# Two draining slots of a software pipeline written out by hand, with a new order on four engines

## Reference, cut to what matters

```python
h = _layernorm(x) * (1 + ca) + sa
# eight times, with weights of the layer:
q, k, v = h @ Wq + bq, h @ Wk + bk, h @ Wv + bv
Q, K = elu(q) + 1, elu(k) + 1
KV, Ksum = (K * v).sum(rows), K.sum(rows)
V = Q * KV / (Q * Ksum + EPS_Z)
h = _layernorm(gelu(V @ Wo + bo) + h, ln1)
h = _layernorm(gelu(gelu(h @ Wf1 + bf1) @ Wf2 + bf2) + h, ln2)
# behind the layers:
x = x + ga * h
h = _layernorm(x) * (1 + cb) + sb
x = x + gb * (shared(h) + sum over the 2 best of 8 experts)
```

## Time and profile before

| | |
|---|---|
| median of 3 runs (lowest, highest) | 519.76 us (519.69, 519.83) |
| profiled execution, its own time | 519.92 us |
| its span, first to last instruction | 518.1 us |
| busy PE / DVE / ACT / POOL | 97% / 82% / 74% / 48% |
| granted TensorE clock, mean | 1.000 |

### The profile page before, as it was taken

The page is one execution under the profiler, slowest core; times in us unless marked ns, Lnnn a source line. Parts: engine busy times, 40 slices in busy tenths (PEclk is TensorE's granted clock), DMA queues, the critical chain, the costliest instruction groups (busy, mean ns, idle before and its releaser), DMA issues.

```text
span 518.1 us, 7999 instructions
## 1 busy us (share of the span) xinstructions
PE 502.8 (97%) x1933; PEld 299.1 (58%) x1933; DVE 423.4 (82%) x1624; ACT 384.7 (74%) x570; POOL 247.1 (48%) x291
## 2 busy tenths in 40 slices
PE   8789999999999999999999999999989999999997
PEld 6345555555555556555555555555555566666664
DVE  5888888988898888888888888898887656876754
ACT  4768888888888888888888888888887753545332
POOL 3445555566556566655556655566655530201000
PEclk9999999999999999999999999999999999999999
DMA  8200010001000000100010001000000000707070
GB/s 246 95 16 1 7 41 15 0 5 41 15 5 20 20 15 5 40 16 0 5 41 15 5 0 41 15 5 20 20 1 1 2 0 13 171 0 184 1 184 20
DMA packets 19527, 17.51 MB, mean 34 GB/s; under 512 B 8605, under 2 KB 14237, under 8 KB 19509
## 3 DMA queue, kind: packets, MB, share of 16 engines
q1 hardware_dynamic: 18644, 16.58, 12.4%
q10 hardware_dynamic: 864, 0.73, 0.4%
HBM read 9.96 MB, written 1.05 MB: 21 GB/s over the span
## 4 chain that ended last, share of the span: by engine, by line
PE 87%; DVE 5%; POOL 3%; issue 2%; ACT 2%; DMA 1%; DVEq 0%; POOLq 0%
PE bank L442 19%; PE bank L433 15%; PE bank L308 12%; PE bank L598 7%; PE bank L455 6%; PE bank L430 5%; PE bank L350 4%; PE bank L355 4%; PE bank L351 4%; PE bank L558 3%; PE bank L557 3%; PE bank L556 3%; DVE hf L1042 1%; PE bank L554 1%; DVE stI L1006 1%
## 5 line engine op out<-in xcount | busy, mean ns | idle before, releaser
L442 PE MATMUL bank<-hid,wf 128*128 128x512 f32 x256 | 120.2, 592 | 0.0
L915 POOL TENSOR_TENSOR rsD<-veD,c_half 128x4 f32<-128x4 f32 x32 | 37.8, 1180 | 118.0 <-DVE veD L1023 118.0
L433 PE MATMUL bank<-x,wf 128*128 128x512 f32 x192 | 93.0, 593 | 0.0
L758 ACT ACTIVATE hid<-bank,vbf 128x512 f32<-128x512 f32 x128 | 77.6, 693 | 1.9 <-PE bank L433 1.9
L442 PEld LDWEIGHTS bank<-hid,wf 128*128 128x128 f32 x256 | 46.1, 190 | 46.6 <-issue 31.3
L433 PEld LDWEIGHTS bank<-x,wf 128*128 128x128 f32 x192 | 35.0, 189 | 33.3 <-issue 16.3
L1113 DVE TENSOR_SCALAR x<-bank,vln 128x256 f32<-128x256 f32 x64 | 31.9, 540 | 23.8 <-PE bank L308 23.8
L1042 DVE TENSOR_SCALAR xhB<-bank,meanB,rsB 128x128 f32<-128x128 f32 x128 | 43.7, 404 | 9.2 <-POOL rsB L915 9.2
L1042 DVE TENSOR_SCALAR xhD<-bank,meanD,rsD 128x128 f32<-128x128 f32 x128 | 43.7, 404 | 7.2 <-POOL rsD L915 2.9
L728 ACT ACTIVATE g<-bank,vbf 128x512 f32<-128x512 f32 x31 | 21.4, 690 | 35.8 <-PE bank L442 35.8
L308 PEld LDWEIGHTS bank<-ident,y 128*128 128x128 f32 x256 | 29.5, 140 | 26.3 <-POOL y L935 12.9
(11 more groups left out here) (175 smaller groups left out, 1087.9 us busy)
## 6 DMA issues: line engine op xcount, KB each, us to landing
wf<-in_w_f SPq DMA_DIRECT2D x16, 256.0 KB, 2.6
hid<-kv_full SPq DMA_DIRECT2D x12, 256.0 KB, 4.2
x<-kv_full SPq DMA_DIRECT2D x9, 256.0 KB, 5.0
wu<-in_w_unit SPq DMA_DIRECT2D x10, 192.0 KB
wqkv<-in_w_qkv SPq DMA_DIRECT2D x7, 192.0 KB, 2.3
x<-in_x SPq DMA_DIRECT2D x4, 256.0 KB, 5.5
qk<-kv_full SPq DMA_DIRECT2D x3, 256.0 KB, 4.9
out<-ot SPq DMA_DIRECT2D x3, 256.0 KB, 2.2
```

Source lines behind the costliest of these rows:

```text
L433: mm = nc.tensor.matmul(ps_ff[j][:], wf1[:, j * P:(j + 1) * P], x2[(c - 2) % CH][:], start=True, stop=True)
L442: mm = nc.tensor.matmul(ps_f0[:], wf2[:, j, :], hid[:, j, :], start=(j == 0), stop=(j == FJ - 1))
L758: nc.scalar.activation(hid[:, j, :], ps_ff[j][:], ACT.Gelu_apprx_tanh, bias=vbf1[:, j:j + 1]).then_inc(h_ready, 1)
L915: nc.gpsimd.tensor_tensor(rs[buf(k, n)][:], ve[buf(k, n)][:], c_half[:], ALU.pow).then_inc(rstd_ready[k], 1)
```

## The change

The last slot of the loop and the two draining slots are no longer written by `slot`:

- ScalarE: the table of Ln, Ln and dd of item 31 come directly behind the gelus of slot 31, with the last norm of item 28 between them (it was at the end of slot 31), then zf; the gelu g2 of item 29, which stood ahead of them, comes behind. The weight splits and the second norm stand at other places of the stream.
- DVE: the end of slot 31 (normalize of B for item 30, and rk) is written behind rk and nck; x2 comes behind vt; y1 of item 31 is added on DVE instead of POOL; the statistics of F come ahead of those of B, those of D for item 29 behind them.
- TensorE: Wo of item 31 goes into ps_v instead of ps_b and stands ahead of ff1 of item 30; y1's transposes go into ps_v, the hidden norm of chunk 0 into ps_b (`fm_bank`); the transposes of y2 (item 29) come behind ff1(0), those of its normalized rows in the next slot, behind the scores; the scores stand within ff1 of item 31; the transposes of y2 of item 30 come behind ff2(1) of item 31, and those of its normalized rows behind ff2(3). All `keep_awake` calls here are gone.
- POOL: three of the roots, the sums, h_lo and the low parts in a new order, without y1.

The diff, without its blank lines:

```diff
@@ -115,6 +115,10 @@
         first_bank = [ps_f0, ps_f1, ps_f0, ps_d]
         gate_bank, up_bank = [ps_k, ps_f1], [ps_b, ps_f0]
+        def fm_bank(c):
+            return ps_v if c else ps_b
         def gates(i):
@@ -504,12 +508,12 @@
             def norm_to_fm(c):
                 pe.wait_ge(normed["F"], c + 1)
                 if c == 0:
-                    pe.wait_ge(kv_ready, NI)
+                    pe.wait_ge(x2_ready, HB * last)
                 if c:
                     pe.wait_ge(cst_ready, c)
                 if c == 2:
                     pe.wait_ge(x_ready, NI + CH)
-                transposes(ps_v, xh["F"], to_fm["F"])
+                transposes(fm_bank(c), xh["F"], to_fm["F"])
             def scores(c):
                 pe.wait_ge(hf_ready, c + 1)
@@ -561,6 +565,7 @@
                 c, u = divmod(i, U)
                 if i == 0:
                     pe.wait_ge(hf_ready, 1)
+                    pe.wait_ge(x2_ready, HB * NI)
                 if c == 0 and i >= FIRST:
                     pe.wait_ge(wu_hi_ready, i - FIRST + 1)
                     pe.wait_ge(wu_lo_ready, i - FIRST + 1)
@@ -578,8 +583,6 @@
             def up(i):
                 c, u = divmod(i, U)
-                if i == 0:
-                    pe.wait_ge(x2_ready, HB * NI)
                 if i == 1:
                     pe.wait_ge(g2_ready, NI)
                 if i >= 2 and i - 2 < U:
@@ -625,15 +628,68 @@
                 gate(0)
                 up(0)
-            slot(NI, 0, LAYERS, {"start": lambda: zf_to_tm(0)})
+            def sum_to_tm(d):
+                pe.wait_ge(y2_ready, d + 1)
+                pe.wait_ge(x_ready, d + CH)
+                transposes(ps_d, y2, to_tm["D"])
+            def rows_to_fm(d):
+                pe.wait_ge(normed["D"], d + 1)
+                transposes(ps_d, xh["D"], to_fm["D"])
+            def inner(f, j):
+                if j == 0:
+                    pe.wait_ge(g2_ready, f)
+                if j == 3:
+                    pe.wait_ge(k_ready, NI)
+                    pe.wait_ge(h_ready, FJ * f)
+                if j == 2:
+                    for h in range(HB):
+                        pe.wait_ge(x2_ready, HB * f + h + 1)
+                        mm = nc.tensor.matmul(half(ps_ff[2], h), wf1[:, 2 * P:3 * P], half(x2[f % CH], h),
+                                              start=True, stop=True)
+                else:
+                    mm = nc.tensor.matmul(ps_ff[j][:], wf1[:, j * P:(j + 1) * P], x2[f % CH][:],
+                                          start=True, stop=True)
+                mm.then_inc(ff1_mm, 1)
+            def outer(f, js):
+                for j in js:
+                    pe.wait_ge(h_ready, FJ * f + j + 1)
+                    mm = nc.tensor.matmul(ps_f0[:], wf2[:, j, :], hid[:, j, :], start=(j == 0), stop=(j == FJ - 1))
+                if j == FJ - 1:
+                    mm.then_inc(ff2_mm, 1)
+            pe.wait_ge(normed["B"], last)
+            transposes(ps_b, xh["B"], to_fm["B"])
+            zf_to_tm(0)
+            pe.wait_ge(v_ready, NI)
             pe.wait_ge(kv_ready, NI)
-            keep_awake(12, ps_v)
-            def awake_0():
-                keep_awake(4, ps_v)
-            slot(NI + 1, 1, LAYERS, {"start": awake_0, "within ff1": lambda: norm_to_fm(0),
-                                     "behind ff2": scores_0, "behind the last norm": unit_0})
+            nc.tensor.matmul(ps_v[:], wo[:], vt[CH - 1][:], start=True, stop=True).then_inc(wo_mm, 1)
+            inner(last - 1, 2)
+            inner(last - 1, 0)
+            pe.wait_ge(y1_ready, NI)
+            transposes(ps_v, y1, to_tm["B"])
+            sum_to_tm(last - 2)
+            inner(last - 1, 1)
+            inner(last - 1, 3)
+            outer(last - 1, (0, 1, 2, 3))
+            pe.wait_ge(normed["B"], NI)
+            transposes(ps_v, xh["B"], to_fm["B"])
+            norm_to_fm(0)
+            inner(last, 2)
+            inner(last, 0)
+            scores_0()
+            rows_to_fm(last - 2)
+            inner(last, 1)
+            inner(last, 3)
+            outer(last, (0, 1))
+            sum_to_tm(last - 1)
+            outer(last, (2, 3))
+            rows_to_fm(last - 1)
+            unit_0()
             for i in range(CH * U):
@@ -765,7 +821,7 @@
                         run(extra, "before the last norm")
                     if j == 3 and has(a) and splits_next(s, c):
                         split_qkv_hi(l + 1)
-                    if j == 3 and has(d) and has(b):
+                    if j == 3 and has(d) and has(b) and has(s + 1):
                         last_norm(c, d)
                         if has(s + 1):
                             act.wait_ge(v_mm, d + 1)
@@ -788,7 +844,7 @@
                 act.wait_ge(to_fm["F"], c + 1)
                 for h in range(HB):
                     b = c * HB + h
-                    ev = nc.scalar.activation(half(hf[c], h), half(ps_v, h), ACT.Identity,
+                    ev = nc.scalar.activation(half(hf[c], h), half(fm_bank(c), h), ACT.Identity,
                                               bias=mod[:, 3, b:b + 1], scale=m1[:, 1, b:b + 1])
                 ev.then_inc(hf_ready, 1)
@@ -846,22 +902,42 @@
                 for u in us:
                     nc.scalar.activation(wu_hi[:, u, 0:2, :], wu[:, u, 0:2, :], ACT.Copy).then_inc(wu_hi_ready, 1)
-            def first_rows():
-                second_norm(0)
-                split_h_hi(0)
-            def last_splits():
-                split_weights_hi(ORDER[7:])
-                scaled(1)
+            def outer_gelu(f):
+                act.wait_ge(ff2_mm, f + 1)
+                nc.scalar.activation(g2[:], ps_f0[:], ACT.Gelu_apprx_tanh, bias=vbf2[:, 0:1]).then_inc(g2_ready, 1)
+            def inner_gelu(f, j):
+                act.wait_ge(ff1_mm, FJ * f + (2, 3, 1, 4)[j])
+                nc.scalar.activation(hid[:, j, :], ps_ff[j][:], ACT.Gelu_apprx_tanh,
+                                     bias=vbf1[:, j:j + 1]).then_inc(h_ready, 1)
+            nc.scalar.preload_act_table_set(LN_SET)
+            act.wait_ge(q_ready, NI)
+            nc.scalar.activation(lden[:], qk[:], ACT.Ln, bias=c_eps[:, 0:1]).then_inc(lden_ready, 1)
+            last_norm(CH - 1, NI - CH)
+            act.wait_ge(lden_ready, NI)
+            nc.scalar.activation(dd[:], lden[:], ACT.Exp, bias=c_lneps[:, 0:1], scale=-1.0).then_inc(dd_ready, 1)
             scaled(0)
-            slot(NI, 0, LAYERS, {"after the first gelu": lambda: split_weights_hi(ORDER[:3]),
-                                "before the last norm": lambda: split_weights_hi(ORDER[3:5]),
-                                "end": lambda: split_weights_hi(ORDER[5:7])})
-            slot(NI + 1, 1, LAYERS, {"start": lambda: norm_rows(0), "after the first gelu": first_rows,
-                                     "before the last norm": last_splits})
-            act.wait_ge(ff2_mm, NI)
-            nc.scalar.activation(g2[:], ps_f0[:], ACT.Gelu_apprx_tanh, bias=vbf2[:, 0:1]).then_inc(g2_ready, 1)
+            outer_gelu(NI - 3)
+            act.wait_ge(wo_mm, NI)
+            nc.scalar.activation(g1[:], ps_v[:], ACT.Gelu_apprx_tanh, bias=vbo[:, 0:1]).then_inc(g1_ready, 1)
+            for j in range(FJ):
+                inner_gelu(NI - 2, j)
+            norm_rows(0)
+            outer_gelu(NI - 2)
+            second_norm(0)
+            split_h_hi(0)
+            split_weights_hi(ORDER[:2])
+            inner_gelu(NI - 1, 0)
+            last_norm(0, NI - 3)
+            for j in range(1, FJ):
+                inner_gelu(NI - 1, j)
+            split_weights_hi(ORDER[2:5])
+            scaled(1)
+            split_weights_hi(ORDER[5:])
+            outer_gelu(NI - 1)
             exponentials(0)
             for i in range(CH * U):
                 c, u = divmod(i, U)
@@ -970,18 +1046,22 @@
                 nc.gpsimd.tensor_tensor(h_lo[c % 2][:], hf[c][:], h_hi[c % 2][:].bitcast(F32),
                                         ALU.subtract).then_inc(h_lo_ready, 1)
-            def first_low_parts():
-                split_h(0)
-                split_weights_lo(ORDER[2:3])
-            slot(NI, 0, LAYERS)
+            def outer_sum(f):
+                pool.wait_ge(g2_ready, f + 1)
+                nc.gpsimd.tensor_tensor(y2[:], g2[:], x2[f % CH][:], ALU.add).then_inc(y2_ready, 1)
+            outer_sum(NI - 3)
             rstd("F", 0)
             norm_bias(0)
-            split_weights_lo(ORDER[:2])
-            slot(NI + 1, 1, LAYERS, {"behind the sum": first_low_parts})
+            rstd("B", NI - 1)
+            rstd("D", NI - 3)
+            outer_sum(NI - 2)
+            split_h(0)
+            split_weights_lo(ORDER[:3])
+            rstd("D", NI - 2)
             split_weights_lo(ORDER[3:6])
-            pool.wait_ge(g2_ready, NI)
-            nc.gpsimd.tensor_tensor(y2[:], g2[:], x2[CH - 1][:], ALU.add).then_inc(y2_ready, 1)
+            outer_sum(NI - 1)
             for i in range(FIRST, CH * U - 2):
```

(51 more changed lines are left out.)

## The result

The changed kernel takes 522.04 us (median of 8 runs, 520.26 to 523.05) against 519.84 for the kernel before in the same series: slower by 0.4%, a small change but clear of the noise (the ratio worked out from all runs is 1.0036, with a 95% interval of 1.0027 to 1.0046; that of the two medians is 1.0042). The forecast was 520.5, in a range of 519.5 to 521.8, with 0.67 for a change too small to be told. The ratio times 519.76 is 521.6 and lies inside that range, the plain median lies above it. The profiled execution has 522.08 us and a span of 520.3, 2.2 more than before.

What follows compares the result with a forecast made beforehand. TensorE, fully busy behind the drain, was taken as the bound, so gate(0)'s start decides: 410.32 against 409.57, +0.75 us, profiled time 520.67, less 0.16 for the median: 520.5, range 519.5 to 521.8.

Steps and rivals of the forecast that it cites:

- The sequence of the drain: TensorE's start times, step by step, from 387.38 to gate(0), forecast at 410.32 against 409.57 before.
- Ln and dd ahead: ScalarE runs them before the other chunk's gelu, so Wo starts on TensorE at 388.31 instead of 390.52.
- y1 met POOL: DVE's add of y1 is stretched by POOL's y2 add, ending at 391.09; TensorE waits 0.24 us.
- the hidden chain of B: Statistics, root, normalize behind y1 end at 396.7, before TensorE asks at 397.23; cover only 0.5 us.
- Where the gained time goes: Time taken out of the drain becomes one 2.6 us TensorE wait for xhD, behind the y2 transposes of 405.04.
- The later start: gate(0), the first gate product behind the drain, starts at 410.32 instead of 409.57: +0.75 us.
- rival 3: TensorE's clock falls in the wait for xhD, unit 0 runs at 1.2 GHz: +2.5 us, 522.2; chance 0.06.
- the removal of these transposes: Drain: 12 and 4 identity transposes counted as needless TensorE time, part of about 3 us that could be taken out.
- The row given for the clock's price: At the kernel's start, the same weight load takes 333 ns at first and 186 later, cited for the lower clock's cost.
- No new wait behind gate(0): From gate(0) to the end, TensorE gets no new wait, costed at nothing; the same 108.5 us remain.

Runs made afterwards that it cites:

- e6: e3 with the drain's old start back (g2 ahead of Ln and dd, x2 ahead of vt, Wo behind ff1(0)), y1 still on DVE: 519.84 us, ratio to before 0.9998.
- e2: Changed kernel with the y2 transposes of item 30 ahead of ff2(0) of item 31, POOL unchanged: 519.15 us, ratio to the kernel before 0.9984.
- e3: Changed kernel with item 30's y2 transposes between ff1(1) and ff1(3), and its root ahead of POOL's third low weight part: 518.53 us, ratio to before 0.9966.
- e1: Changed kernel with 20 identity transposes in TensorE's wait ahead of item 30's last-norm transposes: 520.26 us, ratio to the kernel before 1.0004.
- e4: Kernel before without its 12 and 4 identity transposes in the drain: 520.26 us, a median between two groups of runs, ratio to before 1.0002.
- e8: e3 with the router's sums and weights on DVE behind unit 0's product instead of ahead: 518.10 us, ratio to the kernel before 0.9966.
- e7: Changed kernel with 8 identity transposes at the start of TensorE's wait for xhD: 520.36 us, ratio to the kernel before 1.0009.
- e5: e3 with y1 of item 31 added on POOL again, behind y2 of item 29: 519.50 us, ratio to the kernel before 0.9988.

## Why the prediction was right and where it failed

- **The sequence of the drain: right.** Wo 388.3 forecast, 388.23 found; y1's transposes 391.1, 391.01; xhB 397.23, 397.09; y2 405.04, 404.89; wait 2.6, 2.51; xhD 409.82, 409.71. "Ln and dd ahead" did its work (e6), y1 met POOL as read from the earlier trace rows, and the hidden chain of B stayed hidden: normalize ended at 396.51, 0.6 before it was asked for.
- **"Where the gained time goes": right.** The change turned what it took out into one wait at its end, because the y2 transposes moved behind ff2(1) with only 1.72 us of products as cover for a chain of 4.8. e2 shows it by moving just them, and e3 by moving one weight split as well. The later start came to 0.64 in the profile (0.72 with its lead) and to about 0.5 in the times of e1, against 0.75.
- **The step that failed is rival 3, weighed at 0.06 and left out of the sum: "The array's clock falls in the 2.6 us wait".** Its mechanism was named, and its price of 1.72 came out as 1.69, but its chance was wrong. The profiled execution has the fall, and by their times seven of the eight runs do; the eighth, at 520.26, has the time that e1 gives without it. I had taken the absence of a fall in one trace as evidence, while that trace held no wait longer than 1.53 us behind its first products, and two of its waits in the drain were filled with identity transposes. e1 shows the cause by filling the wait, and e4 that even shorter waits bring the fall in a part of the runs. I also costed the removal of these transposes as pure gain; with their cover gone, the clock fell.
- **That 521.6 lies inside the range is luck.** The range was meant to leave out a fall of the clock, forecast at 522.2. The fall came; it stayed inside because the terms ahead of it came out smaller, about 0.5 instead of 0.75, and because 521.6 goes by the ratio of all runs: the plain median, 522.04, lies outside.
- **The row given for the clock's price did not show it.** The slow weight load of 333 ns stood under a granted clock that shows no change there. The changed kernel's trace has the comparison: a weight load of the same size (128x128, for the products of 410.54) takes 0.34 us at a granted clock of 0.50 and 0.19 at 1.00.
- **No new wait behind gate(0): right** for TensorE in the changed kernel. In e3, where gate(0) comes earlier still, a wait of 0.31 appears at 412.78: on DVE the router's sums and weights, which begin with ScalarE's exponentials at 410.37 and end at 412.13, stand ahead of unit 0's product. e8 takes them out of its way.

## What to carry to other kernels

When the order is changed on the engine that sets the end, follow each chain that leaves it and comes back, and ask how much of its work lies between; time saved ahead of a chain whose start was pushed back comes out as one wait behind it. A wait of TensorE has two prices, its length and the clock behind it: a trace at full clock that has no long wait says nothing about one, and transposes of the identity in a wait are cover, not waste. The fall comes in some executions and not in others, so look at all the single times and not at one profile. Move the start of the chain before adding cover.

## What the runs showed of the hardware that was not expected

- Counted by the single times, with one profile for each kernel: the clock fell in seven of eight runs behind 2.51 us idle, in about five of 12 behind 1.31 and 0.64 us, 0.6 apart (e4), in none to two of 11 behind 1.63 us (e7), in none of 12 behind 1.33 us (e2), and in none of the 12 of e1, with 0.32 us idle behind the identity transposes. In the two profiled falls it came 0.1 us (changed kernel) and 0.4 us (e4) behind the restart, not in the wait, and lasted 3.4 us, so that only useful work was slowed, by 1.6 to 1.7 us.
- A second place of that kind is in the fill: in the profiled executions of e4 and e5 the clock falls at 29.6 and 29.3 us, and they are 1.0 us longer. Ahead of it TensorE waits 0.9 and 0.73 us, 0.66 apart, until 28.9. The kernel before has the same two waits, and its profile shows no fall there.
- Not only adds are stretched when DVE and POOL meet. The cast of the selection matrix, 0.72 us in the kernel before, took 1.75 in the changed kernel from 400.01, and ended 0.54 behind the end of POOL's h_lo (xs_lo in the rows, 399.92 plus 1.30). It lay in slack here. In e2 even an operation on four columns was held for 0.54.
